# Two graph layers on one core: another order of work in the last two steps

## The reference

```python
q, k, v = heads(x @ Wq + bq), heads(x @ Wk + bk), heads(x @ Wv + bv)      # 12 heads of 32
s = q @ k.T / sqrt(32) + beta * adj;  s = where(adj > 0, s, -9e15)
h = layernorm(x + softmax(s) @ v, eps=1e-5)                               # h0
z = h
for l in range(2):                                                        # the two inner layers
    a = softmax(z @ z.T / sqrt(384)) * adj
    a = a / (a.sum(-1) + 1e-10)
    c = (a * upper) @ (z @ Wl[l].T + bl[l]) + diag(a) * (z @ Ws[l].T + bs[l]) \
        + (a * lower) @ (z @ Wr[l].T + br[l])
    z = relu(layernorm(c, eps=1e-12) * g[l] + b[l])
out = layernorm(h + z, eps=1e-5)
```

## Time and profile before

| | |
|---|---|
| median of three runs | 1292.63 us |
| profiled execution | 1295.08 us |
| its span, first to last instruction | 1293.4 us |
| TensorE busy | 1261.8 us, 98% |
| VectorE busy | 984.8 us, 76% |
| ScalarE busy | 629.7 us, 49% |
| GpSimd busy | 366.7 us, 28% |
| mean granted TensorE clock | 0.990 |

### The profile page before, as it was taken

One profiled execution on the slowest core, in us unless ns is written; L12 is line 12 of the kernel. 1 busy time (PEld: TensorE's weight loads), 2 busy tenths in 40 slices (PEclk: granted clock), 3 DMA queues, 4 the chain that ended last, 5 costly groups with the idle time before them and its releaser, 6 DMA issues.

```text
span 1293.4 us, 34503 instructions
## 1 busy us (share of the span) xinstructions
PE 1261.8 (98%) x13844; PEld 1168.9 (90%) x13844; DVE 984.8 (76%) x2672; ACT 629.7 (49%) x1329; POOL 366.7 (28%) x398
## 2 busy tenths in 40 slices
PE   8999999999999999999999999999999999999885
PEld 8999999999999999999999999999999999999774
DVE  5777778777778777878777878777878777787765
ACT  5544554544554544554534554445545445545432
POOL 3222323322323232323222323222323222323211
PEclk9999999999999999999999999999999999999997
DMA  8211111011110111110111110111110111110000
GB/s 273 82 40 57 57 57 30 29 56 57 57 57 24 35 56 57 57 57 18 41 57 56 57 57 7 51 57 57 57 49 9 57 57 57 57 35 12 26 13 25
DMA packets 52206, 66.32 MB, mean 51 GB/s; under 512 B 17744, under 2 KB 38352, under 8 KB 51920
## 3 DMA queue, kind: packets, MB, share of 16 engines
q1 hardware_dynamic: 52048, 64.12, 16.3%
HBM read 38.54 MB, written 12.58 MB: 40 GB/s over the span
## 4 chain that ended last, share of the span: by engine, by line
PE 96%; DVE 2%; issue 1%; ACT 1%; POOL 0%; DMA 0%; POOLq 0%; ACTq 0%; SPq 0%; DVEq 0%
PE bank L359 25%; PE bank L361 23%; PE bank L360 23%; PE bank L550 7%; PE bank L462 4%; PE bank L499 4%; PE bank L447 3%; PE bank L428 3%; PE bank L475 2%; PE bank L485 2%; PE bank L530 1%; DMA late<-in_w_qk 0%; DVE ln_six L1012 0%; DVE probs L900 0%; POOL probs L1184 0%
## 5 line engine op out<-in xcount | busy, mean ns | idle before, releaser
L359 PE MATMUL bank<-w_hi,hT_hi 128*128 128x384 f32 x1158 | 405.2, 350 | 1.9 <-DVE hlr L966 1.0
L361 PE MATMUL bank<-w_hi,hT_lo 128*128 128x384 f32 x1158 | 390.3, 337 | 0.0
L360 PE MATMUL bank<-w_lo,hT_hi 128*128 128x384 f32 x1158 | 390.1, 337 | 0.0
L359 PEld LDWEIGHTS bank<-w_hi,hT_hi 128*128 128x128 f32 x1158 | 218.4, 189 | 6.6 <-issue 2.2
L360 PEld LDWEIGHTS bank<-w_lo,hT_hi 128*128 128x128 f32 x1158 | 219.0, 189 | 0.0
L361 PEld LDWEIGHTS bank<-w_hi,hT_lo 128*128 128x128 f32 x1158 | 218.5, 189 | 0.0
L966 DVE TENSOR_TENSOR hlr<-bank,rows 128x384 f32<-128x384 f32 x256 | 142.0, 556 | 79.4 <-PE bank L361 76.6
L1197 POOL TENSOR_TENSOR ln_rstd<-ln_var,minus_half 128x2 f32<-128x2 f32 x128 | 98.7, 771 | 350.6 <-DVE ln_var L1018 131.5
L1184 POOL TENSOR_TENSOR probs<-probs,row_max 128x768 f32<-128x768 f32 x64 | 94.3, 1475 | 275.9 <-DVE row_max L906 275.9
L981 DVE TENSOR_TENSOR late<-bank,rows 128x384 f32<-128x384 f32 x128 | 71.3, 557 | 123.5 <-PE bank L361 123.5
L359 PE MATMUL bank<-xT_hi,w_hi 128*128 128x256 f32 x558 | 158.8, 285 | 0.0
(11 more groups left out here) (101 smaller groups left out, 2349.0 us busy)
## 6 DMA issues: line engine op xcount, KB each, us to landing
v_halves<-v_stage SPq DMA_DIRECT2D x128, 99.0 KB, 2.3
xT_in<-in_xT SPq DMA_DIRECT2D x32, 384.0 KB, 3.5
x_in<-in_x SPq DMA_DIRECT2D x32, 384.0 KB, 4.1
out<-late SPq DMA_DIRECT2D x32, 384.0 KB, 2.4
late<-in_w SPq DMA_DIRECT2D x7, 576.0 KB, 5.7
adj_in<-in_adj SPq DMA_DIRECT2D x32, 96.0 KB, 3.9
adjT_in<-in_adjT SPq DMA_DIRECT2D x64, 48.0 KB, 3.2
rows<-in_vectors SPq DMA_DIRECT2D x1, 1536.0 KB, 8.0
```

The source lines that it names most:

```text
L359: nc.tensor.matmul(o, l_hi, r_hi, start=first and n == 0, stop=False)
L360: nc.tensor.matmul(o, l_hi, r_lo, start=False, stop=False)
L361: done = nc.tensor.matmul(o, l_lo, r_hi, start=False, stop=final and n == last)
```

## The change

For units 0 to 29 the order on each engine stays. `h0` gets three buffers instead of two, `c1` two instead of one (the second in columns 7D to 9D of `late`), and the store's semaphore is one for each c1 buffer.

Step 30 (`next_to_last` on every engine): on TensorE `transpose_probs` and `attend` come before `transpose_z`, and `transpose_h` goes ahead of the last side projection of layer 1. On DVE both `max_scores` come early, `heads_out` comes before `zT_low`, and the pieces of the FINAL unit 29 are spread between the others. On ACT both `exp_scores` and `take_pT` come before `normalize_inner`, and the FINAL unit's normalization comes last.

Step 31 (`last`): the two tiles of unit 31 go one behind the other. Tile 0's `mix(0)` comes before tile 1's projections of layer 0, and so on through layer 1 and the end. Eight banks are used, since no EARLY or MID unit needs them. Statistics, roots, shifts, maxima, diagonals, masks and normalizations are done for one tile at a time. `take_zT`, `split_zT` and `zT_low` become, for each tile, three pieces of 128 columns, each with its own count (`last_take_z`, `last_low`), and the first left product of layer 1 starts on the first piece (`last_left_and_gram`). The FINAL stage of unit 31 is in the same lists (`end`), with a store for each tile; step 32 is empty but for these stores.

The diff, cut to the orders and to those new functions that are more than one tile of an old one:

```diff
+    def h_slot(self, stage):
+        return (self.s + stage) % 3
...
+        h0 = sb("h0", [P, 3, T, D])
         hT = sb("hT", [P, T, KC, P])
         hT_hi = sb("hT_hi", [P, T, KC, P], F32R)
...
+        c1 = [late[:, at:at + 2 * D].rearrange("p (t d) -> p t d", t=T) for at in (4 * D, 7 * D)]
         self_turned = late[:, 6 * D:7 * D]
-        c = [c0, c1]
...
         CTX_BANKS = [[bank[5], bank[4]], [bank[6], bank[7]]]
+        LAST = UNITS - 1
+        LAST_U_BANK = [bank[5], bank[6]]
+        LAST_HLR_BANKS = [[bank[4], bank[0], bank[4], bank[0]], [bank[6], bank[7], bank[6], bank[7]]]
+        LAST_AT_BANK = bank[3]
+        LAST_TILE_BANKS = [bank[4], bank[5]]
+        LAST_SELF_BANKS = [[bank[1], bank[1]], [bank[0], bank[0]]]
+        LAST_CTX_BANKS = [[bank[2], bank[3]], [bank[1], bank[3]]]
...
                     load_x(st, MID + 1)
-                if st.has(FINAL):
+                if st.has(FINAL) and st.unit(FINAL) == LAST:
+                    for t in range(T):
+                        need(sp, y_ready, st.count(FINAL, 2, t + 1))
+                        sp.dma_start(out[LAST][:, t], context(LAST, 1)[:, t]).then_inc(y_stored[LAST % 2], 16)
+                elif st.has(FINAL):
                     need(sp, y_ready, st.count(FINAL, 2, 2))
-                    sp.dma_start(out[st.unit(FINAL)], c1).then_inc(y_stored, 16)
+                    sp.dma_start(out[st.unit(FINAL)], context(st.unit(FINAL), 1)).then_inc(y_stored[st.slot(FINAL)], 16)
                 if st.has(EARLY):
...
+            def next_to_last(st):
+                gram(st, 0)
+                project_sides(st, 0)
+                transpose_e(st, 0)
+                project_self(st, 0, 0)
+                project_self(st, 0, 1)
+                mix(st, 0)
+                transpose_probs(st)
+                attend(st)
+                transpose_z(st)
+                gram(st, 1)
+                project_side(st, 1, 0, LEFT)
+                project_side(st, 1, 0, RIGHT)
+                project_side(st, 1, 1, LEFT)
+                transpose_h(st)
+                project_side(st, 1, 1, RIGHT)
+                transpose_e(st, 1)
+                project_self(st, 1, 0)
+                project_self(st, 1, 1)
+                mix(st, 1)
...
+            def last_left_and_gram(st, t):
+                if t == 0:
+                    need(pe, ctx_ready[1], st.count(FINAL, 2, 1))
+                else:
+                    need(pe, hlr_ready, st.count(LATE, 8, 5))
+                for kc in range(KC):
+                    need(pe, z_hi, KC * t + kc + 1)
+                    need(pe, z_lo, KC * t + kc + 1)
+                    done = product(LAST_HLR_BANKS[1][2 * t + LEFT][:, 0:D],
+                                   [((hT_hi[:, t, kc, :], hT_lo[:, t, kc, :]), weight(W_LATE + 3 + LEFT, kc))],
+                                   first=kc == 0, final=kc == KC - 1)
+                    if kc == 0:
+                        last_gram(st, t)
+                done.then_inc(hlr_psum, 1)
...
+            def last_gram(st, t):
+                need(pe, z_taken, KC * t + KC)
+                if t == 0:
+                    need(pe, hlr_ready, st.count(LATE, 8, 3))
+                for kc in range(KC):
...
+            def last_mix(st, l, t):
+                need(pe, hlr_ready, st.count(LATE, 8, 4 * l + 2 * t + 2))
+                if l == 0:
+                    need(pe, aT_ready, st.count(LATE, 2, 1))
+                else:
+                    need(pe, tile_aT, t + 1)
+                if l == 1 and t == 0:
+                    need(pe, self_ready, st.count(LATE, 4, 2))
+                if l == 1 and t == 1:
+                    need(pe, ctx_ready[0], st.count(LATE, 2, 2))
+                for m in (LEFT, RIGHT):
+                    for g in range(GRAPHS):
+                        rows_of, o = slice(g * N, (g + 1) * N), turn(t, g)
+                        done = nc.tensor.matmul(LAST_CTX_BANKS[l][t][o * N:(o + 1) * N, 0:MW], aT[rows_of, t, m, rows_of],
+                                                hlr[rows_of, t, m, 0:MW], start=m == LEFT, stop=m == RIGHT)
+                done.then_inc(ctx_psum, 1)
...
+            def last(st):
+                gram(st, 0)
+                last_side(st, 0, 0, LEFT)
+                last_side(st, 0, 0, RIGHT)
+                transpose_e(st, 0)
+                last_self(st, 0, 0)
+                last_mix(st, 0, 0)
+                last_side(st, 0, 1, LEFT)
+                last_side(st, 0, 1, RIGHT)
+                last_self(st, 0, 1)
+                last_transpose_z(st, 0)
+                last_mix(st, 0, 1)
+                last_left_and_gram(st, 0)
+                last_side(st, 1, 0, RIGHT)
+                last_transpose_e(st, 0)
+                last_self(st, 1, 0)
+                last_transpose_z(st, 1)
+                last_mix(st, 1, 0)
+                last_left_and_gram(st, 1)
+                last_side(st, 1, 1, RIGHT)
+                last_transpose_e(st, 1)
+                last_self(st, 1, 1)
+                last_mix(st, 1, 1)
...
+            def next_to_last(st):
+                exp_gram(st, 0)
+                exp_scores(st, 0)
+                exp_scores(st, 1)
+                scale_self(st, 0)
+                scale_turned(st, 0)
+                take_pT(st)
+                normalize_inner(st)
+                take_zT(st)
+                split_zT(st)
+                exp_gram(st, 1)
+                normalize_h(st)
+                take_hT(st)
+                split_hT_tile(st, 0)
+                scale_self(st, 1)
+                split_hT_tile(st, 1)
+                scale_turned(st, 1)
+                normalize_final(st)
...
+            def last_take_z(st, t):
+                act.wait_ge(z_psum, t + 1)
+                need(act, u_psum, st.count(LATE, 2, 1))
+                need(act, hTlo_ready, st.count(LATE, 4, 2))
+                need(act, self_psum, st.count(LATE, 4, t + 1))
+                for kc in range(KC):
+                    nc.scalar.activation(hT[:, t, kc, :], LAST_Z_BANKS[t][:, kc * P:(kc + 1) * P], ACT.Relu,
+                                         bias=b0_col[:, kc:kc + 1], scale=g0_col[:, kc:kc + 1]).then_inc(z_taken, 1)
+                    act.wait_ge(z_taken, KC * t + kc + 1)
+                    nc.scalar.activation(hT_hi[:, t, kc, :], hT[:, t, kc, :], ACT.Copy).then_inc(z_hi, 1)
...
+            def last(st):
+                exp_gram(st, 0)
+                scale_self(st, 0)
+                last_z(st, 0)
+                last_take_z(st, 0)
+                scale_turned(st, 0)
+                last_exp(st, 0)
+                last_z(st, 1)
+                last_take_z(st, 1)
+                scale_self(st, 1)
+                last_exp(st, 1)
+                normalize_final(st)
+                scale_turned(st, 1)
+                last_normalize(st, 0)
+                last_normalize(st, 1)
...
+            def next_to_last(st):
+                mask_scores(st, 0, 3)
+                make_ctx(st, FINAL, 1)
+                max_gram(st, 0)
+                mask_scores(st, 3, 4)
+                max_scores(st, 0)
+                sides_bias(st, 0, 0, LEFT)
+                sides_bias(st, 0, 0, RIGHT)
+                take_diag(st, 0)
+                max_scores(st, 1)
+                sides_bias(st, 0, 1, LEFT)
+                sides_bias(st, 0, 1, RIGHT)
+                mask_aT(st, 0)
+                stats_inner(st, FINAL, 1, ln3_den, ln3_stats, ln3_aggr, ln3_eps, ln3_six, ln3_mv, ln3_var)
+                self_bias(st, 0)
+                final_center(st, 0)
+                make_ctx(st, LATE, 0)
+                stats_inner(st, LATE, 0, ln1_den, ln1_stats, ln1_aggr, ln1_eps, ln1_six, ln1_mv, ln1_var)
+                final_center(st, 1)
+                shift(st, LATE, ln1_mv, ln1_rstd, ln1_shift, ln1_rs, ln1_sh)
+                heads_out(st)
+                final_scale(st, 0)
+                final_scale(st, 1)
+                zT_low(st)
+                max_gram(st, 1)
+                stats_outer(st)
+                final_add(st, 0)
+                sides_bias(st, 1, 0, LEFT)
+                sides_bias(st, 1, 0, RIGHT)
+                shift(st, MID, ln0_mv, ln0_rstd, ln0_shift, ln0_rs, ln0_sh)
+                final_add(st, 1)
+                take_diag(st, 1)
+                sides_bias(st, 1, 1, LEFT)
+                final_stats(st)
+                sides_bias(st, 1, 1, RIGHT)
+                mask_aT(st, 1)
+                shift(st, FINAL, ln2_mv, ln2_rstd, ln2_shift, ln2_rs, ln2_sh)
+                self_bias_tile(st, 1, 0)
+                hT_low_tile(st, 0)
+                self_bias_tile(st, 1, 1)
+                hT_low_tile(st, 1)
...
+            def last_stats(st, l, t, s_den, s_six, s_mv, s_eps, six, mv, var):
+                need(dve, den_ready, st.count(LATE, 6, 3 * l + (1 if t == 0 else 3)))
+                nc.vector.scalar_tensor_tensor(out=den_sq[:, l, t:t + 1], in0=den[:, l, t:t + 1], scalar=EPS_INNER,
```

(126 more changed lines are left out.)

269 lines of the change are left out of this document (218 added, 51 removed).

## The result

The changed kernel takes 1282.67 us, the median of four runs from 1281.89 to 1283.67, against 1292.64 for the kernel before: a ratio of 0.9919 with a 95% interval of 0.9902 to 0.9937. Run again beside the experiments it took 1282.89 us, ratio 0.9918 (0.9905 to 0.9932). So it is about 10.5 us faster. I had forecast 15.0 us and a range from 1275.5 to 1282.0; the sign was right, the size too large, and the time lies above the range.

The account below looks back on a forecast made before the run. TensorE was taken as busy throughout except the last 90 us, where waits for z and a low clock cost time. Gains 4.1 + 8.6 + 3.1 = 15.8, less 0.8, gave 15.0 us: 1277.6 us, range 1275.5 to 1282.0.

Parts of the forecast that it names:

- Part A: Unit 30's step: probabilities' transposes and attention fill the idle 5.54 us before z's transposes; gain 4.1 us, bounds 0 to 4.6.
- my first rival: TensorE's clock falls in unit 30's step, with 1.5 us of work between 1223.0 and 1227.7: 3.4 us, 1281.0; chance 0.22.
- The time of z: Unit 30's step: z's transposes start at 1224.5 instead of 1225.04, as DVE's chain loses max_scores(1) and gains final_center(1).
- the cover for the probabilities: Unit 30's step: second tile's probabilities ready at 1216.3, TensorE free of mix at 1219.5, so 3 us of cover.
- Part B: Unit 31 from gram to last product: each tile's work covers the other's chain; 26.3 us against 34.9, gain 8.6 us.
- the mix of one tile: Unit 31: tile 1's layer 0 mix follows transposes ending at 1251.6 and ends at 1252.35.
- the gaps that I had forecast: Unit 31: five TensorE gaps of 0.25 to 1.15 us, 2.0 us in sum, the largest before tile 1's layer 1.
- The price of a chunk on ACT: Unit 31's z pieces: two ACT passes over 128 columns and a wait, 0.70 us per chunk, bounded between 0.36 and 1.1.
- rival (3): Short gaps hold TensorE's clock at 0.50 through the whole last unit: 1297.8 us; chance 0.03.
- Rival (2): DVE's queue becomes the bound of the last unit, operations and waits costing 10% more: 2.5 us, 1280.1; chance 0.12.
- Part C: Tail after the last product: only tile 1 is left, 11.5 us instead of 14.6; gain 3.1 us.
- 0.8 held back for hops: Whole sum: some 16 hops between engines at 0.05 us in doubt, taken off the 15.8 us gain.

Follow-up runs that it names:

- made alone: The new order in unit 30's step only, old order for unit 31 and the end, against the kernel before: 1293.41 us, ratio 0.9989.
- the fillers: Changed kernel plus 12 unread matmuls in unit 30's step, 8 before z's transposes and 4 after: 1281.58 us, ratio 0.9909 to the kernel before.
- mixes of 0.87 us: Changed kernel with the RIGHT half of each of unit 31's four mixes left out: 1282.16 us, ratio 0.9912 to the kernel before.
- the next reordering: Changed kernel with 6 and 4 unread matmuls in unit 30's step, z's transposes by tile, and final_center of the second tile moved later: 1280.80 us.
- one filler: Changed kernel with only 8 unread matmuls before z's transposes, or only 4 after them, in unit 30's step: 1282.04 and 1282.08 us.

## Why the prediction was wrong

**Part A, 4.1 us forecast, 0.6 in the profile, 1.4 when made alone.** Two steps of it failed.
The clock: I gave its fall, my first rival, a chance of 0.22 and priced it at 3.4 us. It fell in all four profiles of this order without fillers. (A wait of 2.31 us stood before z where I had said about 1.5.) The argument against it, that a fall needs more than 4 us with no matmul at all, was taken from the two falls that the trace happened to show. Here 2.31 us of idle time, 0.84 of transposes and 1.41 of idle time were enough. It cost 1.8 to 2.0 us of the step's time by the fillers, less than my 3.4.
The time of z: I let it come 0.54 us earlier, and it came 0.31 later (18.02 us after gram, 17.71 before). Some 0.3 of the 0.54 were to come because max_scores(1) leaves the stretch ahead of shift. But it had stood under POOL's root, which shift must wait for, and cost nothing there; what replaced it, a scalar_tensor_tensor, stretched the root from 0.69 to 1.00 us. Before, then after:

```profile
1222.51 0.94 DVE L906 TENSOR_REDUCE row_max<-probs 128x12 f32<-128x768 f32 x1
1222.67 0.69 POOL L1197 TENSOR_TENSOR ln_rstd<-ln_var,minus_half 128x2 f32<-128x2 f32 x1 [1.62 <-DVE ln_var L1018]
1223.39 0.16 DVE L866 SCALAR_TENSOR_TENSOR ln_shift<-ln_mv,ln_rstd 128x2 f32<-128x2 f32 x1
```

```profile
1221.33 0.61 DVE L1312 SCALAR_TENSOR_TENSOR late<-late,ln_mv,rows 128x384 f32<-128x384 f32 x1
```

I knew of that price, and used it in the tail, but not here. The other 0.25 of the 0.54 are a sum that was too short: I took 1.4 us from shift to z's transposes, which took 1.65 before and 1.64 after. That is 0.85 us of the step, and transposes, copies and splits took 0.5 more than I had summed: first product forecast 20.4 us after gram, measured 21.75.
Right in A: the cover for the probabilities (ready at 1215.4, needed at 1218.3), and that transposes and attention fit into the gap with 0.45 us of wait.

**Part B, 8.6 forecast, 7.0 measured.** The mis-sized term is the mix of one tile: I took 0.75 us, half of the old one, and it takes 1.51 (1.45 to the next instruction). Three stand before the last product, 2.1 us more than I had summed. A second term was short too: TensorE's other work, its gaps and mixes aside, takes 23.4 us where I had 22.0. Of these 1.4 us 0.95 are layer 1 of the two tiles, 5.65 and 5.95 us, summed as 5.25 and 5.4. Against both stand the gaps that I had forecast, 2.0 us in sum, of which only 0.16 came. With mixes of 0.87 us the unit still takes 27.25 us, not my 26.3; the gaps are then 1.3 us and the other work is the same, so it is this work and not the chain of z that I had summed too short. The price of a chunk on ACT, unknown from the trace, was right: two passes, 0.70 us a chunk (starts at 1254.93, 1255.63 and 1256.32). The clock stayed at 1.00 in the whole unit, so rival (3) fell as argued. Rival (2) is half true at most: DVE is not the bound. But it has next to no gap from 1257.6 to 1264.3, and with the short mixes 0.8 us of waiting appears before tile 1's first product, whose subtraction there stands right behind self_bias; the other 0.5, before tile 0's, is the chain through ACT.

**Part C, 3.1 forecast, 3.3 measured.** Right. The small store lands in 1.9 us where the whole one takes 2.4; I had taken no gain for it, and from its issue to the end of the span it is 2.4 us instead of my 2.75. The estimate from the Trainium skill's fixed cost (DMA: Bandwidth & Descriptors, Anatomy of one DMA) was 0.4 us less, and the trace agrees with this difference within 0.1. It does not agree with the 2.0 us of fixed cost, which that section gives for transfers issued by GpSimd: here SyncE issues them, and the 192 KB take less than that altogether.

**The sum and the range.** 3.5 us too much in A, 1.6 in B, 0.2 too little in C, and 0.8 held back for hops. The range ended at 1282.0, because it took in the rivals one at a time: the fall of the clock alone, 1281.0, or 2.5 us of longer queues, 1280.1. What came was the fall of the clock together with a later z and dearer mixes, and no rival had the price of a mix. One reading of the earlier trace rows was loose, and nothing rests on it: the first slice of the busy line, too, is below 9 tenths.

## What to carry to other kernels

When one of two interleaved tiles is worked off alone, look whether the two shared the engine side by side: halving the matmuls of a mix did not shorten it (1.51 and 1.53 us). A gain that comes as earlier work behind a thin stretch has to be priced with the clock of what follows, and here a dozen matmuls whose result nobody reads gave 1.8 to 2.0 us in the profile, the next reordering 0.6. Before counting an operation as removed from a chain, look what it ran beside; under a wait that stays it was free.

## What the runs showed of the hardware

In the profiles TensorE's clock fell from 2.4 to 1.2 GHz after stretches that held some work: 0.84 us of transposes between idle times of 2.31 and 1.41 us did not keep it, 1.6 to 2.05 us of extra matmuls in the first and 1.06 in the second did. Once low, it stayed so for about 6.8 us in the changed kernel (1225.3 to 1232.1, by the clock of the slices at both ends) and for about 3.4 with one filler.

In 64-row tiles the time of a group is that of the fullest quadrant, whatever the order in the program: 1.53 us for sixteen matmuls on four quadrants, 1.51 for eight on two, 2.81 for sixteen on two, 0.87 for four on two.

POOL's root of 128x2 takes 1.00 us beside a DVE scalar_tensor_tensor of 384 columns; it takes 0.69 with DVE idle, and also beside DVE's tensor_reduce.
